# A two-layer decoder on one core: the delta rule's gates in one batch, and another order in its last eight steps

## The chip, the cores and the metric

The kernel runs on one core of one Trainium2 chip. The time is the device time of one launch in microseconds. A profiled execution gives the trace that the rows below are taken from.

## The reference, cut to what matters

Sixteen sequences of 112 tokens and 256 columns go through two decoder layers. The change lies in the first part of the first layer, a gated delta rule with eight heads of 128 columns:

```python
mixed = causal_conv4(x @ qkv_w.T)            # q, k, v: 8 heads x 128
z, bb, aa = x @ z_w.T, x @ b_w.T, x @ a_w.T
beta = sigmoid(bb)
alpha = exp(-exp(A_log) * softplus(aa + dt_bias))
for t in range(T):                           # per sequence and head
    S = S * alpha[t]
    S = S + outer(k[t], (v[t] - k[t] @ S) * beta[t])
    o[t] = q[t] @ S
o = o * rsqrt(mean(o * o) + 1e-6) * norm_w * silu(z)
out = o.reshape(16, 112, 1024) @ out_w.T
```

Behind it come a cross attention, a mixture of eight experts, then in the second layer an attention, a cross attention and a feed-forward part.

## The kernel before, in words

The step over time is turned into matrix products. For each sequence and head, a 112 x 112 matrix of decays (gamma: exp of differences of running sums of the log gates, with log beta added) multiplies k k^T to give N0 and k q^T to give QG. With the inverse of the unit triangular matrix of N0 the output follows. The inverses of the 14 x 14 diagonal blocks (paired to 28 x 28) are worked out on VectorE; the rest is solved by a short series of products, called M, R, Y1, Y2, Y3.

The work is cut into 32 units: eight heads, each with four groups of four sequences (G = 4, 448 columns). Unit u belongs to head u // 4 and group u % 4. The keys part runs eight units ahead (AHEAD = 8) of the solving part. So there is a start, in which units 0 to 7 get their keys, a main loop of 24 steps (u = 0 to 23), each of which solves unit u, finishes the tail of unit u - 1, prepares the values of unit u + 1 and the keys of unit u + 8, and eight last steps (u = 24 to 31) without a keys part. Step 31 begins the cross attention in place of unit 32's values. Every engine's order is written out by hand, and engines wait for each other by semaphores with counts; an engine takes its instructions in that order, so whatever stands behind a waiting instruction waits too. SP issues nearly all DMAs in one queue, with the same effect.

What the steps of the prediction touch:

- The start (gdn_pe, gdn_act, gdn_dve, gdn_pool): for each group, TensorE transposes the normalised rows (start_pe_turn), ScalarE copies them (start_act_copy), TensorE projects 16 gate columns (start_pe_gates), ScalarE copies these (start_act_gates, L455), TensorE turns them back to tokens (start_pe_tokens). Then for a batch of two groups: gate input on VectorE (L361, L362), soft plus on ScalarE (L461 to L468, with a load of the table for Ln and another for Exp behind it), gate output on VectorE (L370, L373), running sums on TensorE (L393, L394), their copy and DMA to memory on ScalarE (L400, L402), and the bias of the sums on VectorE (L381).
- The decays of a unit a: SP fetches its running sums, spread to 112 partitions (cumulative, L1208); logs(a) on GpSimd adds the bias and takes the minimum with zero (L1147, four instructions, into a tile of their own); ScalarE takes the exponential (L838); gammas(a) on GpSimd masks it (L1156); VectorE multiplies it in (N0 at L976, QG at L982).
- The convolutions of keys, queries and values are three instructions each on VectorE (L956) behind ScalarE's tap (L830, L833, L844).
- Inversion and exchange of a head: SP writes N0's diagonal blocks (L1219), gathers them (L1241), VectorE inverts (rows, L536 to L567), SP exchanges the inverses (L1252 to L1264), two joins on GpSimd (join parts 0 and 2, L580) alternate with two on VectorE (parts 1 and 3, L592, L600), and SP writes and spreads the joined blocks (L1270, L1277). Product M of the head's first unit (L672) waits for them. For heads 1 to 7 this goes on inside the steps: joins in the step two ahead of the head's first (u = 2, 6, ..., 26), and in the last eight steps part 0 stands in step 25.
- A step's tail: ScalarE squares the output (L869), GpSimd takes the root (L1160, L1162), ScalarE scales (scale_out, L876), TensorE transposes (L719), VectorE gates (L1018), TensorE projects (L728), VectorE adds to x (L1025). Values: projections L608 (slot 6 for v, slot 8 for z), transposes L657, copy to W0 L852, gate z L992.

## Time and profile before

| | us |
|---|---|
| median of 3 runs | 1888.66 |
| lowest, highest | 1886.35, 1888.81 |
| the profiled execution's own time | 1888.68 |
| its span in the trace | 1887.0 |
| TensorE busy (matmul) | 1806.5 (96%) |
| VectorE busy | 1174.6 (62%) |
| ScalarE busy | 709.8 (38%) |
| GpSimd busy | 669.4 (35%) |

The span runs from the first to the last instruction of the trace; the execution's own time is 1.68 us longer. A busy share is a mean over all stages: the delta rule ends at about 563 us, and what a change in it is worth is read from the stage that it lies in. An idle time in brackets is that of the engine just before the row, with what ended it. In the trace's names, big_a, big_b, h_w, w, expert_w and small are tiles that several stages share; ps is PSUM.

### The profile page before, as it was taken

Reading aid. Unit: us, or ns where it says so; the run is one execution under the profiler, and the core shown is the slowest. Engines: PE = TensorE matmul, PEld = TensorE weight load, DVE = VectorE, ACT = ScalarE, POOL = GpSimd, SP = SyncE. Lnnn points to the kernel's source line nnn. Section 1 sums busy time; section 2 is a strip of 40 time slices with the busy share of each in tenths; the row PEclk is TensorE's granted clock in tenths of the full one; section 3 lists DMA queues with packets and bytes.
Section 4 is the critical chain, followed back from the end, with each engine's and each line's share of the span. In section 5 each row is a group of like instructions: output and inputs, shape, how many; then the busy total and the mean of one; then the engine's idle time right before and its main releaser. Section 6 shows DMA issues by size and latency. Waiting matters only on the chain.

```text
span 1887.0 us, 39461 instructions
## 1 busy us (share of the span) xinstructions
PE 1806.5 (96%) x14800; PEld 1302.7 (69%) x14800; DVE 1174.6 (62%) x3215; ACT 709.8 (38%) x1887; POOL 669.4 (35%) x758
## 2 busy tenths in 40 slices
PE   6679999999889999999999999999999999999999
PEld 3357777776666666665445666666659979889698
DVE  5588888887656677677766667666665234243332
ACT  4124444444345555553001455655632222122221
POOL 3344443443216666674000376676624000000000
PEclk9879999999999999999999999999999999999999
DMA  6312212121022001010000000010040000000000
GB/s 195 53 33 49 39 34 43 37 42 26 13 79 71 25 27 36 26 35 11 1 1 1 10 29 20 20 29 20 11 179 1 3 7 1 10 1 1 10 1 10
DMA packets 98717, 58.61 MB, mean 31 GB/s; under 512 B 77801, under 2 KB 90465, under 8 KB 97761
## 3 DMA queue, kind: packets, MB, share of 16 engines
q1 hardware_dynamic: 98368, 56.03, 11.1%
q8 instruction: 120, 1.97, 0.4%
q14 instruction: 69, 0.56, 0.1%
q10 hardware_dynamic: 160, 0.06, 0.0%
HBM read 50.55 MB, written 5.51 MB: 30 GB/s over the span
## 4 chain that ended last, share of the span: by engine, by line
PE 81%; issue 5%; POOL 5%; DVE 4%; ACT 3%; DMA 1%; SPq 1%; DVEq 0%; POOLq 0%; ACTq 0%
PE ps L2582 18%; PE ps L1566 6%; PE ps L608 6%; PE ps L2454 5%; PE ps L1588 5%; PE ps L2114 5%; PE ps L1604 4%; PE ps L1643 4%; PE ps L1622 4%; PE ps L2660 3%; PE ps L728 2%; POOL w L580 2%; PE ps L1709 2%; PE ps L1575 2%; PE ps L1654 1%
## 5 line engine op out<-in xcount | busy, mean ns | idle before, releaser
L2027 POOL TENSOR_TENSOR h_w<-h_w 125x336 int32<-125x336 int32 x384 | 335.9, 904 | 210.4 <-ACT h_w L1808 210.4
L1912 DVE CUSTOM_DVE_ANT_0 h_w<-ps,h_w 112x375 f32<-112x375 f32 x512 | 263.3, 544 | 0.6 <-issue 0.3
L956 DVE SCALAR_TENSOR_TENSOR big_b<-ps,taps,big_b 128x444 f32<-128x444 f32 (+2 forms) x288 | 194.0, 674 | 74.9 <-ACT big_b L830 47.9
L1808 ACT ACTIVATE h_w<-ps 125x336 f32<-125x336 f32 x512 | 197.7, 468 | 21.7 <-PE ps L1588 21.7
L275 POOL TENSOR_TENSOR rstd<-var_eps,minus_half 112x4 f32<-112x4 f32 x12 | 12.2, 1015 | 406.5 <-DVE var_eps L262 406.5
L1588 PEld LDWEIGHTS ps<-h_w 32*125 32x125 f32 x3072 | 96.0, 183 | 62.1 <-issue 61.3
L1588 PE MATMUL ps<-h_w 32*125 32x112 f32 x3072 | 118.0, 282 | 7.8 <-DVE h_w L1912 5.5
L1921 DVE TENSOR_TENSOR h_w<-h_w,ps 128x112 f32<-128x112 f32 x128 | 34.7, 271 | 141.6 <-PE ps L1575 141.6
L1566 PE MATMUL ps<-h_w 32*112 32x375 f32 x1024 | 121.1, 519 | 0.8 <-DVE h_w L1912 0.8
L608 PE MATMUL ps<-h_w,w 128*128 128x448 f32 x256 | 110.3, 554 | 4.6 <-ACT h_w L852 4.6
L608 PE MATMUL ps<-h_w,kq_w 128*128 128x448 f32 x256 | 113.7, 569 | 0.0
L2114 PE MATMUL ps<-expert_w,big_a 128*112 128x512 f32 x256 | 113.6, 596 | 0.0
L1604 PE MATMUL ps<-h_w 125*32 125x112 f32 x3072 | 101.3, 264 | 0.5 <-POOL h_w L2027 0.4
L2454 PE MATMUL ps<-xT,w 128*128 128x448 f32 x256 | 98.0, 541 | 1.1 <-DVE big_a L2469 1.1
L1156 POOL TENSOR_TENSOR big_a<-big_a,minus_upto 112x448 f32<-112x448 f32 x32 | 36.4, 1136 | 148.5 <-ACT big_a L838 148.5
L2225 DVE SCALAR_TENSOR_TENSOR x<-ps,small,x 112x256 f32<-112x256 f32 x128 | 61.9, 483 | 37.0 <-PE ps L2114 34.0
L2114 PEld LDWEIGHTS ps<-expert_w,big_a 128*112 128x112 f32 x256 | 43.9, 177 | 57.5 <-issue 48.0
L1931 DVE TENSOR_TENSOR h_w<-h_w 125x336 f32<-125x336 f32 x128 | 81.9, 640 | 2.5 <-ACT h_w L1808 2.4
L2454 PEld LDWEIGHTS ps<-xT,w 128*128 128x128 f32 x256 | 48.6, 191 | 46.8 <-issue 44.9
L1604 PEld LDWEIGHTS ps<-h_w 125*32 125x32 f32 x3072 | 70.2, 109 | 15.6 <-issue 1.2
L2582 PE MATMUL ps<-big_b,h_w 128*128 128x224 f32 x384 | 79.1, 353 | 0.0
L2582 PE MATMUL ps<-big_a,h_w 128*128 128x224 f32 x384 | 78.5, 353 | 0.0
(360 smaller groups left out, 3728.9 us busy)
## 6 DMA issues: line engine op xcount, KB each, us to landing
h_w<-in_h SPq DMA_DIRECT2D x2, 4096.0 KB, 17.0
kq_w<-in_ctxT SPq DMA_DIRECT2D x16, 375.0 KB, 3.4
h_w<-in_ctxT SPq DMA_DIRECT2D x16, 375.0 KB, 3.3
big_a<-decays SPq DMA_DIRECT2D x16, 196.0 KB, 3.2
w<-decays SPq DMA_DIRECT2D x16, 196.0 KB, 3.1
h_w<-in_mask SPq DMA_DIRECT2D x16, 164.1 KB, 3.3
kq_w<-in_kq_w SPq DMA_DIRECT2D x8, 256.0 KB, 3.7
w<-in_vz_w SPq DMA_DIRECT2D x8, 256.0 KB, 3.6
```

The lines of the kernel that those rows point to most:

```text
L608: ins = pe.matmul(ps[:, bank, 0:GT], w[:, c, :], c_in[:, c, :], start=(c == 0), stop=(c == KD - 1))
L956: dve.scalar_tensor_tensor(p3(dst)[:, :, i:], p3(ps[:, bank, 0:GT])[:, :, 0:T - i], k.taps[:, h, n, TAPS - 1 - i:TAPS - i], p3(dst)[:, :, ...
L1566: pe.matmul(ps[0:T, score_bank(Q, r), 0:S2], k.Qz[n % 2][rows, z, m, :], k.Kx[n % 2][rows, z, m, :], start=True, stop=True).then_inc(s["S" ...
L1588: ins = pe.matmul(ps[0:CK, turned_bank(Q, r), c * T:(c + 1) * T], k.Kx[n % 2][rows, z, m, c * CK:(c + 1) * CK], k.Qx[Q % 2][rows, :], star ...
L1604: ins = pe.matmul(ps[32 * r:32 * r + 32, 6, q * T:(q + 1) * T], k.Vx[n % 2][:, c, 4 * q + r, :], k.PTx[(4 * Q + r) % RING][:, c * T:(c + 1 ...
L1808: act.activation(k.PTx[(4 * Q + r) % RING], ps[0:CK, turned_bank(Q, r), 0:NC * T], ACT.Exp).then_inc(s["exp"], 1)
L1912: dve.tensor_tensor_reduce(k.masked[r % 2], ps[0:T, score_bank(Q, r), 0:S2], k.mask_add[n % 2], -1.0, 3.0e38, ALU.add, ALU.min, k.neg_max[ ...
L1931: dve.tensor_tensor(P, P, k.mask_I[n % 2], ALU.min).then_inc(s["weights0"], 1)
L2027: pool.tensor_tensor(P.bitcast(I32), P.bitcast(I32), k.mask_I[n % 2], ALU.mult).then_inc(s["weights"], 1)
L2114: ins = pe.matmul(ps[0:T, bank, :], k.moe_xT[g % 2][:, c, j * T:(j + 1) * T], k.expert_w[:, c, e * D:(e + 2) * D], start=(c == 0), stop=(c ...
L2454: ins = pe.matmul(k.ps[:, 2 + 2 * n + m % 2, 0:GT], k.w12[:, n, c, m * 128:(m + 1) * 128], k.xT[:, c, :], start=(c == 0), stop=(c == KD - 1))
L2582: ins = pe.matmul(ps[:, product_bank(p, m), FIRST_HALF], lhsT, rhs, start=(c == 0), stop=(c == QT - 1))
```

## The change

The gates of all sixteen sequences are worked out in one batch. All four groups' turns, copies and gate projections come ahead of unit 0's first tap on ScalarE, and gate input, soft plus, gate output, running sums, their write and the bias run once on 128 columns instead of twice on 64. ScalarE takes unit 0's query tap behind the soft plus. The logs of a unit are one tensor_tensor and one tensor_scalar over 448 columns, in place in the fetched sums, instead of four tensor_scalars of 112 columns into another tile. In the start GpSimd takes logs(a + 1) ahead of gammas(a). SP's fetch waits for the exponential of the unit two back instead of its logs.

In the last eight steps TensorE takes z's projection, Y2, v's projection, the tail's transposes and M behind Y1, where it took v's projection, the transposes, Y2, z's projection and M. ScalarE takes A ahead of the scaling and z ahead of v. VectorE takes less, the gate and the R sum ahead of the values' convolution, M and z.

The diff, cut to its core:

```diff
-BATCH = 2 * G
+ALL = B * HEADS
...
 
 def turn_banks(g):
-    return (5, 0) if g == 1 else (3, 4)
+    return (5, 0) if g % 2 else (3, 4)
...
-def start_dve_gate_in(dve, k, s, b):
+def start_dve_gate_in(dve, k, s):
     (y, t1, t2, bb), _, _, _, _ = start_tiles(k)
-    dve.wait_ge(s["ba_t"], 2 * b + 2)
-    if b == 0:
-        dve.wait_ge(s["c_ba"], 48)
-    for g in (2 * b, 2 * b + 1):
+    dve.wait_ge(s["c_ba"], 48)
+    for g in range(NG):
+        dve.wait_ge(s["ba_t"], g + 1)
         ba = k.ps[0:T, gate_bank(g), GT:GT + G * 16].rearrange("p (g c) -> p g c", g=G)
-        at = slice(G * (g % 2), G * (g % 2) + G)
-        dve.tensor_tensor(y[:, b, at, :], ba[:, :, HEADS:], k.dt_bias[:, :].unsqueeze(1).to_broadcast([T, G, HEADS]), ALU.add)
-        ins = dve.tensor_copy(bb[:, b, at, :], ba[:, :, 0:HEADS])
+        at = slice(G * g, G * g + G)
+        dve.tensor_tensor(y[:, at, :], ba[:, :, HEADS:], k.dt_bias[:, :].unsqueeze(1).to_broadcast([T, G, HEADS]), ALU.add)
+        ins = dve.tensor_copy(bb[:, at, :], ba[:, :, 0:HEADS])
     ins.then_inc(s["ba_in"], 1)
...
+def start_dve_gate_out(dve, k, s):
     (y, t1, t2, bb), _, _, _, _ = start_tiles(k)
-    at = slice(BATCH * b, BATCH * b + BATCH)
-    dve.wait_ge(s["soft_plus"], nth(b, 5, 4))
-    dve.scalar_tensor_tensor(t2[:, b], y[:, b], 0.0, t1[:, b], ALU.max, ALU.add).then_inc(s["gates"], 1)
-    dve.wait_ge(s["gates"], nth(b, 3, 0))
+    dve.wait_ge(s["soft_plus"], 4)
+    dve.scalar_tensor_tensor(t2, y, 0.0, t1, ALU.max, ALU.add).then_inc(s["gates"], 1)
+    dve.wait_ge(s["gates"], 1)
     dve.wait_ge(s["setup_act"], 1)
-    dve.scalar_tensor_tensor(k.gate_rows[:, 1, b], t2[:, b].rearrange("p s h -> p h s"), -1.0,
-                             k.decay[:, :].unsqueeze(2).to_broadcast([T, HEADS, BATCH]), ALU.mult, ALU.mult).then_inc(s["gates"], 1)
...
+def start_dve_bias(dve, k, s):
 
     (y, t1, t2, bb), _, _, _, _ = start_tiles(k)
-    dve.wait_ge(s["cum_ps"], 2 * b + 1)
-    dve.scalar_tensor_tensor(k.gate_rows[:, 0, b], bb[:, b].rearrange("p s h -> p h s"), -1.0,
-                             k.ps[0:T, 6, 0:BATCH * HEADS].rearrange("p (h s) -> p h s", h=HEADS), ALU.mult, ALU.subtract).then_inc(s["gates"], 1)
-
-
-def start_pe_cum(pe, k, s, b):
-
-    pe.wait_ge(s["gates"], nth(b, 3, 1))
-    if b:
-        pe.wait_ge(s["cum_sb"], b)
-    else:
-        pe.wait_ge(s["ba_in"], 1)
-    g = k.gate_rows[:, 1, b].rearrange("p h s -> p (h s)")
-    pe.matmul(k.ps[0:T, 6, 0:BATCH * HEADS], k.upto[:, :], g, start=True, stop=True).then_inc(s["cum_ps"], 1)
-    pe.matmul(k.ps[0:BATCH * HEADS, 5, 0:T], g, k.upto[:, :], start=True, stop=True).then_inc(s["cum_ps"], 1)
-
-
-def start_act_cum(act, k, s, b):
-
-    act.wait_ge(s["cum_ps"], 2 * b + 2)
-    act.activation(k.cum_rows[b], k.ps[0:BATCH * HEADS, 5, 0:T], ACT.Copy).then_inc(s["cum_sb"], 1)
-    act.wait_ge(s["cum_sb"], b + 1)
-    act.dma_start(k.cum_d[b].rearrange("h s t -> (h s) t"), k.cum_rows[b]).then_inc(s["cum_w"], 16)
+    dve.wait_ge(s["cum_ps"], 2)
+    dve.wait_ge(s["soft_plus"], 5)
+    dve.scalar_tensor_tensor(k.gate_rows[:, 0], bb.rearrange("p s h -> p h s"), -1.0,
+                             k.ps[0:T, 6, 0:ALL].rearrange("p (h s) -> p h s", h=HEADS), ALU.mult, ALU.subtract).then_inc(s["gates"], 1)
+
+
+def start_pe_cum(pe, k, s):
+
+    pe.wait_ge(s["gates"], 2)
+    g = k.gate_rows[:, 1].rearrange("p h s -> p (h s)")
+    pe.matmul(k.ps[0:ALL, 5, 0:T], g, k.upto[:, :], start=True, stop=True).then_inc(s["cum_ps"], 1)
+    pe.matmul(k.ps[0:T, 6, 0:ALL], k.upto[:, :], g, start=True, stop=True).then_inc(s["cum_ps"], 1)
+
+
+def start_act_cum(act, k, s):
+
+    act.wait_ge(s["cum_ps"], 1)
+    act.activation(k.cum_rows, k.ps[0:ALL, 5, 0:T], ACT.Copy).then_inc(s["setup_act"], 1)
+    act.wait_ge(s["setup_act"], 2)
+    act.dma_start(k.cum_d.rearrange("h s t -> (h s) t"), k.cum_rows).then_inc(s["cum_w"], 16)
...
+def start_act_soft_plus(act, k, s):
...
 def gdn_pe(pe, k, s):
...
     start_pe_turn(pe, k, s, 0)
     start_pe_gates(pe, k, s, 0)
     start_pe_turn(pe, k, s, 1)
+    start_pe_tokens(pe, k, s, 0)
+    start_pe_gates(pe, k, s, 1)
+    start_pe_turn(pe, k, s, 2)
+    start_pe_tokens(pe, k, s, 1)
+    start_pe_gates(pe, k, s, 2)
     keys(0, 0)
-    start_pe_turn(pe, k, s, 2)
-    start_pe_gates(pe, k, s, 1)
+    start_pe_turn(pe, k, s, 3)
+    start_pe_tokens(pe, k, s, 2)
+    start_pe_gates(pe, k, s, 3)
     keys(0, 2)
-    start_pe_tokens(pe, k, s, 0)
-    start_pe_tokens(pe, k, s, 1)
-    start_pe_turn(pe, k, s, 3)
+    start_pe_tokens(pe, k, s, 3)
     keys(1, 0)
     keys(0, 4)
     pe.wait_ge(s["c_gdn"], 96)
-    start_pe_cum(pe, k, s, 0)
-    start_pe_gates(pe, k, s, 2)
+    start_pe_cum(pe, k, s)
     keys(1, 2)
-    start_pe_gates(pe, k, s, 3)
-    start_pe_tokens(pe, k, s, 2)
-    start_pe_tokens(pe, k, s, 3)
     keys(0, 10)
     keys(1, 4)
     keys(2, 0)
     keys(1, 10)
     keys(2, 2)
-    start_pe_cum(pe, k, s, 1)
...
         solve(u, "Y1")
         if more:
+            values(u + 1, 8)
+            solve(u, "Y2")
             values(u + 1, 6)
+            tail(u - 1, 2)
+            solve(u + 1, "M")
         else:
             pe.wait_ge(s["sz"], UNITS)
             cross_head_pe(pe, k, s, 0, 0)
-        tail(u - 1, 2)
-        solve(u, "Y2")
-        if more:
-            values(u + 1, 8)
-            solve(u + 1, "M")
+            solve(u, "Y2")
+            tail(u - 1, 2)
         solve(u, "Y3")
...
 def gdn_act(act, k, s):
...
-            act.wait_ge(s["logs"], a + 1)
+            act.wait_ge(s["logs"], 2 * a + 2)
             if a:
                 act.wait_ge(s["gam"], a)
-            act.activation(k.gamma, k.soft[0:T, :, :].rearrange("p g t -> p (g t)"), ACT.Exp).then_inc(s["gamma"], 1)
+            act.activation(p3(k.gamma), k.cum[a % 2], ACT.Exp).then_inc(s["gamma"], 1)
...
     start_act_gates(act, k, s, 0)
     start_act_copy(act, k, s, 1)
+    start_act_gates(act, k, s, 1)
+    start_act_copy(act, k, s, 2)
+    start_act_gates(act, k, s, 2)
+    start_act_copy(act, k, s, 3)
+    start_act_gates(act, k, s, 3)
     act.wait_ge(s["c_gdn"], 96)
     keys(0, 0)
-    start_act_copy(act, k, s, 2)
-    start_act_gates(act, k, s, 1)
+    start_act_soft_plus(act, k, s)
     keys(0, 2)
-    start_act_soft_plus(act, k, s, 0)
-    keys(1, 0)
-    start_act_cum(act, k, s, 0)
-    start_act_copy(act, k, s, 3)
+    start_act_cum(act, k, s)
     act.wait_ge(s["setup_pool"], 1)
     exp_table()
-    start_act_gates(act, k, s, 2)
+    keys(1, 0)
     keys(1, 2)
     keys(0, 3)
-    start_act_gates(act, k, s, 3)
     keys(1, 3)
-    start_act_soft_plus(act, k, s, 1)
     keys(2, 0)
-    exp_table()
     keys(2, 2)
-    start_act_cum(act, k, s, 1)
     keys(2, 3)
...
-        more = is_unit(u + 1)
+        solve(u, "A")
         scale_out(u - 1)
-        solve(u, "A")
-        if more:
+        if is_unit(u + 1):
+            values(u + 1, 8)
             values(u + 1, 6)
-            values(u + 1, 8)
             solve(u + 1, "R")
...
 def gdn_dve(dve, k, s):
...
-    start_dve_gate_in(dve, k, s, 0)
+    start_dve_gate_in(dve, k, s)
     keys(0, 3)
-    start_dve_gate_out(dve, k, s, 0)
+    start_dve_gate_out(dve, k, s)
     for a in range(1, AHEAD + 1):
         for slot in (2, 4, 3, 10):
             if a == 1 and slot == 2:
-                start_dve_bias(dve, k, s, 0)
+                start_dve_bias(dve, k, s)
             elif a == 1 and slot == 4:
                 keys(1, 3)
-            elif a == 3 and slot == 2:
-                start_dve_bias(dve, k, s, 1)
-            if a == 1 and slot == 10:
-                start_dve_gate_in(dve, k, s, 1)
-            elif a == 2 and slot == 2:
-                start_dve_gate_out(dve, k, s, 1)
...
+        solve(u, "less")
         tail(u - 1, 3)
-        solve(u, "less")
+        if not more:
+            cross_head_dve(dve, k, s, 0, 0)
+        solve(u, "R")
         if more:
             values(u + 1, 7)
+            solve(u + 1, "M")
             values(u + 1, 9)
-            solve(u + 1, "M")
-        else:
-            cross_head_dve(dve, k, s, 0, 0)
-        solve(u, "R")
...
 def gdn_pool(pool, k, s):
...
-        b, first = g // 2, G * (g % 2)
-        if a < NG:
-            pool.wait_ge(s["gates"], 3 * (b + 1))
+        if a == 0:
+            pool.wait_ge(s["gates"], 3)
         pool.wait_ge(s[f"cum_in{a % 2}"], 16 * (a // 2 + 1))
-        if a:
-            pool.wait_ge(s["gamma"], a)
-        for j in range(G):
-            ins = pool.tensor_scalar(k.soft[0:T, j, :], k.cum[a % 2][:, j, :], k.gate_rows[:, 0, b, h, first + j:first + j + 1], 0.0,
-                                     ALU.add, ALU.min)
-        ins.then_inc(s["logs"], 1)
+        cum = k.cum[a % 2]
+        pool.tensor_tensor(cum, cum, k.gate_rows[:, 0, h, G * g:G * g + G].unsqueeze(2).to_broadcast([T, G, T]), ALU.add).then_inc(s["logs"], 1)
+        pool.wait_ge(s["logs"], 2 * a + 1)
+        pool.tensor_scalar(cum, cum, 0.0, None, ALU.min).then_inc(s["logs"], 1)
...
     for a in range(AHEAD):
+        logs(a + 1)
         gammas(a)
-        logs(a + 1)
...
 def gdn_sp(sp, k, s, a):
...
-        first = G * (g % 2)
-        if unit in (0, 2):
-            sp.wait_ge(s["cum_w"], 16 * (g // 2 + 1))
+        if unit == 0:
+            sp.wait_ge(s["cum_w"], 16)
         if unit >= 2:
-            sp.wait_ge(s["logs"], unit - 1)
-        sp.dma_start(k.cum[unit % 2], k.cum_d[g // 2, h, first:first + G].unsqueeze(0).to_broadcast([T, G, T])).then_inc(s[f"cum_in{unit % 2}"], 16)
+            sp.wait_ge(s["gamma"], unit - 1)
+        sp.dma_start(k.cum[unit % 2], k.cum_d[h, G * g:G * g + G].unsqueeze(0).to_broadcast([T, G, T])).then_inc(s[f"cum_in{unit % 2}"], 16)
```

## Rows read from the trace of the kernel before

**Rows 1.** The page, part 4: chain that ended last, by engine.

```profile
PE 81%; issue 5%; POOL 5%; DVE 4%; ACT 3%; DMA 1%; SPq 1%; DVEq 0%; POOLq 0%; ACTq 0%
```

**Rows 2.** Windows: stretch, length, busy PE, PEld, DVE, ACT, POOL, clock, DMA.

```profile
0.00:118.00 118.00, 73.75 (x297) 44.91 (x298) 69.14 (x155) 31.57 (x60) 43.05 (x56) 0.84 0.42 106
118.00:467.00 349.00, 344.64 (x2287) 249.57 (x2286) 294.85 (x537) 149.78 (x474) 150.53 (x176) 1.00 0.20 38
467.00:546.00 79.00, 71.74 (x505) 53.72 (x503) 46.17 (x88) 31.63 (x112) 13.93 (x14) 1.00 0.09 19
```

**Rows 3.** Timeline, start: start us, us, engine line op, names [idle before].

```profile
20.82 2.10 DVE L956 SCALAR_TENSOR_TENSOR big_b<-ps,taps,big_b 128x444 f32<-128x444 f32 x3 [1.41 <-ACT big_b L830]
...
29.24 0.49 ACTq L402 DMA_DIRECT2D decays<-silu  x1
...
35.19 2.60 POOL L1147 TENSOR_SCALAR soft<-big_a,small 112x112 f32<-112x112 f32 x4 [12.60 <-DMA big_a<-decays]
...
38.30 0.52 ACT L455 ACTIVATE big_b<-ps 16x448 f32<-16x448 f32 x1
...
52.59 2.56 POOL L1147 TENSOR_SCALAR soft<-big_a,small 112x112 f32<-112x112 f32 x4 [8.62 <-issue]
...
66.05 0.61 DVE L976 TENSOR_TENSOR h_w<-ps,big_a 112x448 f32<-112x448 f32 x1
...
87.86 0.43 SPq L1208 DMA_DIRECT2D big_a<-decays  x1
...
91.13 2.56 POOL L1147 TENSOR_SCALAR soft<-big_a,small 112x112 f32<-112x112 f32 x4 [20.03 <-DMA big_a<-decays]
...
111.94 1.76 PE L672 MATMUL ps<-expert_w,h_w 112*112 112x84 f32 x8 [0.66 <-DMA expert_w<-joined]
...
117.95 0.76 PE L686 MATMUL ps<-big_a 112*84 112x84 f32 x8
```

**Rows 4.** Lines by form, GpSimd: count, busy us, mean ns, idle before.

```profile
L1147 POOL TENSOR_SCALAR soft<-w,small 112x112 f32<-112x112 f32 x64 | 41.2, 662 | 0.0
...
L1156 POOL TENSOR_TENSOR big_a<-big_a,minus_upto 112x448 f32<-112x448 f32 x32 | 36.4, 1136 | 148.5 <-ACT big_a L838 148.5
...
L2034 POOL TENSOR_SCALAR h_w<-h_w 112x375 f32<-112x375 int32 x16 | 24.0, 1500 | 1.4
...
L1160 POOL TENSOR_SCALAR var_eps<-var_eps 112x4 f32<-112x4 f32 x32 | 8.0, 251 | 123.8 <-ACT xn L869 123.3
```

**Rows 5.** Timeline: loop step u = 2 with a join, and the next.

```profile
152.52 2.58 POOL L1147 TENSOR_SCALAR soft<-w,small 112x112 f32<-112x112 f32 x4
...
159.43 1.14 ACT L876 ACTIVATE xn<-ps,rstd 112x128 f32<-112x128 f32 x4 [0.58 <-POOL rstd L1162]
...
163.28 1.04 PE L630 MATMUL ps<-big_b 128*112 128x112 f32 x8 [0.49 <-DVE big_b L956]
```

**Rows 6.** Windows and timeline of the undisturbed late step 28.

```profile
512.39:523.75 11.36, 10.30 (x74) 7.70 (x73) 5.49 (x10) 4.60 (x19) 1.26 (x2) 1.00 0.01 1
...
513.92 1.74 PE L608 MATMUL ps<-h_w,w 128*128 128x448 f32 x4 [0.77 <-ACT h_w L852]
...
515.95 0.60 PE L719 MATMUL ps<-ident,xn 112*128 112x112 f32 x4 [0.29 <-ACT xn L876]
```

**Rows 7.** Timeline: the joins of head 7 in the last eight steps.

```profile
487.13 2.88 POOL L580 TENSOR_TENSOR w<-w 128x1372 f32<-128x1372 f32 x1 [6.50 <-issue]
...
502.06 1.68 SPq L1277 DMA_DIRECT2D expert_w<-joined  x4
...
507.27 0.93 PE L672 MATMUL ps<-expert_w,h_w 112*112 112x84 f32 x8
```

**Rows 8.** Timeline: TensorE after 5.6 us idle, and in the loop.

```profile
58.48 1.84 PE L630 MATMUL ps<-big_b 128*112 128x112 f32 x8 [5.63 <-DVE big_b L956]
...
60.10 3.22 PE L608 MATMUL ps<-h_w,kq_w 128*128 128x448 f32 x4
...
148.23 1.04 PE L630 MATMUL ps<-big_b 128*112 128x112 f32 x8
```

More of the change, by code:

```diff
@@ L151, in memory @@
     k.On = k.xn[:, 0:2, :].rearrange("p a b -> p (a b)")
[L152 to L153 removed]
+    k.gate_rows = k.small[:, 0:8, :].rearrange("p a b -> p (a b)").rearrange("p (n h s) -> p n h s", n=2, h=HEADS)
+    k.cum_rows = k.silu[:, :, :].rearrange("p a b -> p (a b)")[:, 2 * GT - T:2 * GT]
     k.gate_cols = [k.big_b[0:16, n, :] for n in (3, 5)]
@@ L303, in start_tiles @@
     flat = k.silu[0:T, :, :].rearrange("p a b -> p (a b)")
-    n = 2 * BATCH * HEADS
-    gates = [flat[:, i * n:(i + 1) * n].rearrange("p (b s h) -> p b s h", b=2, s=BATCH) for i in range(4)]
+    n = ALL
+    gates = [flat[:, i * n:(i + 1) * n].rearrange("p (s h) -> p s h", h=HEADS) for i in range(4)]
     mean_var = flat[:, 4 * n:4 * n + 2 * B].rearrange("p (s c) -> p s c", c=2)
@@ L427, in start_pe_gates @@
         pe.wait_ge(s["c_ba"], 48)
-    turned = g + 1 if g < 2 else NG
-    pe.wait_ge(s["lnT_act"], turned)
-    pe.wait_ge(s["lnT_dve"], turned)
+    pe.wait_ge(s["lnT_act"], g + 1)
+    pe.wait_ge(s["lnT_dve"], g + 1)
     for c in range(KD):
```

35 lines of the change are left out of this document (16 added, 19 removed).

## The prediction, made before the changed kernel ran

> **What bounds the kernel now.** I read the chain of work that ended last first: four fifths of it are TensorE's [rows 1], so only what keeps TensorE waiting can be won or lost. The busy time by stretch then says where that is [rows 2]. From 0 to 118 us TensorE works 73.75 of 118 us: the start. From 118 to 467 us, in the 24 steps of the main loop, it works 344.64 of 349 us. From 467 to 546 us, the last eight steps of the delta rule, 71.74 of 79 us. Behind 563 us the change touches nothing. So the reader is to see three places: a start that is bound by waits, a loop that has a few tenths to give, and a tail with 7 us of waits.
>
> In the start the timeline shows the chain [rows 3]: key convolution of unit 0 at 20.82, running sums written out at 29.24, their read back and the first logs at 35.19. Unit 2's logs wait until 52.59 for the second batch of gates (8.62 us idle). The fourth N0 comes at 66.05; then the blocks go through memory, the inversion and the exchange, which SP's queue works off in order, so that the sums of unit 6 are fetched only at 87.86 and GpSimd stands still for 20.03 us until 91.13. The first big product starts at 111.94.
>
> **The change, part 1: one batch of gates in the start.** It removes one pass of gate input, soft plus, two activation table loads, gate output, running sums and a DMA out and in, all on engines that wait in that stretch, and the 8.62 us wait with it. It costs a later first pass. All four groups are now turned and projected before ScalarE taps unit 0's keys: three more groups at some 3.4 us each (gate product, ScalarE's copy of it, copies of the next group; a ScalarE copy is 0.52 [rows 3]). By my walk ScalarE is through with them at about 29 us and the key convolution of unit 0 (2.10) runs at 29.6 instead of 20.82. Behind it on VectorE stands the gate input (31.7); on ScalarE the soft plus (32.6 to 35.2) now stands ahead of unit 0's query tap, and on VectorE the query convolution, which waits for that tap, stands ahead of the gate output. So the output comes at 38, the sums are written at 39.6, and the first logs run at 45 instead of 35.19: 10 us later. From the write at 29.24 to these logs it is 5.95 us now [rows 3]; I take 5.5 in a quieter queue.
>
> What comes after catches up: no second batch, so logs of unit 2 at about 51 (now 52.59). From there VectorE sets the pace (two convolutions of 2.10 and two products of 0.61 a unit, 5.4 us) and the fourth N0 comes at 68 instead of 66.05. Inversion and exchange are unchanged and carry this on: fetch of unit 6's sums at about 89.7 against 87.86, its logs 91.13 plus 1.9.
>
> **Part 2: GpSimd's order and SP's wait.** logs(a+1) now stands ahead of gammas(a). While the sums arrive in time this costs nothing, and twice they don't. Gammas of unit 5, done long before the 20 us wait now, would stand behind logs of unit 6. N0 and the kept product of unit 5 with them, VectorE's joins for head 0 behind these: 1.3 us more, so the first big product at 115.2 against 111.94. The second time is logs of unit 8, whose fetch stands behind the joined blocks in SP's queue: gammas of unit 7, and so the product that TensorE needs for R of step 0, come 5 us later than now. SP's fetches wait for the exponential of the unit two back instead of its logs, as the sums are now changed in place; in the loop the fetch then lands over 10 us ahead of its use, since SP is held by N0 of the unit before anyway. Sum for the start: about +5 us at step 0, +3 at best, +9 at worst (see the price of the new logs).
>
> **Part 3: the logs themselves.** Four tensor_scalars of 112 columns (2.56 us together at 52.59 [rows 3]) become a tensor_tensor and a one-input tensor_scalar on 448 columns. The first has its row: same shape, 1136 ns [rows 4]. The second isn't in the trace. From below it can't cost less than one of today's quarters, 662 ns; from above, L2034 (two operations, one input, 375 columns) took 1500 ns, which is 1.79 us for 448. I take 1.14, the row of the same width with one operation on each element. So 2.28, bounds 1.80 to 2.93. The Trainium skill ("GPSIMD Engine Reference", "3.1 Elementwise — side-by-side cycle accounting") says that a one-input body of up to two operations runs at 1.03 cycles an element against about 2.6 with two inputs; by that the second would cost about as little as the lower bound. From 4 to 375 columns L1160 and L2034 differ by 1249 ns [rows 4], 3.4 ns a column, which speaks for the upper bound at two operations; no row has one operation on many columns of one input.
>
> In the loop this counts only where the joins are: logs lie between two joins, and the root behind them releases ScalarE, which waited 0.58 us for it (159.43), and TensorE, which waited 0.49 us (163.28) [rows 5]. Such a step comes for heads 1 to 6: 6 x -0.28 = -1.7 us, bounds 6 x -0.58 = -3.5 and 6 x +0.37 = +2.2. In the other steps GpSimd waits for ScalarE: zero; its cover would be gone only with some 3 us more a step.
>
> **Part 4: the last eight steps.** In an undisturbed step TensorE works 10.30 of 11.36 us [rows 6], and waits twice: 0.77 us with the value projection for ScalarE's copy of the step before (513.92), and 0.29 us with the transposes for the scaled output (515.95). With the pipeline's drain at both I count 1.35. The new order puts the z projection and Y2 ahead of these two; walking all queues with the durations of such a step, I find both waits gone and the tightest remaining one (the gated output ahead of the output projection) 0.4 us early, so the step is 10.0 us. Six step starts, from step 25's to step 31's, could gain 8.1 us.
>
> But two are lost to the joins of head 7. In step 24 VectorE now has its convolution behind the R sum, so the inversion's end slips by 2.6 us, while the steps are shorter. On GpSimd the first join (487.13, 2.88 us [rows 7]) then runs 489.8 to 492.7, and step 25's root is queued behind it: transposes in step 26 wait 3.2 us. Then the last join stands behind z's product on VectorE, and the joined blocks, spread by SP at 502.06 now with TensorE asking at 507.27 [rows 7], land at 507.7 where TensorE asks at 505.8: 1.9 us. 8.1 - 5.1 = 3.0, with 0.2 in the last step -3.2 us; bounds -5 and -1.
>
> **Sum.** +5.0 - 1.7 - 3.2 = +0.1 us. The profiled execution took 1888.68 us with a span of 1887.0, the median is 1888.66: the same base. Forecast 1889 us. Less than 0.2% (3.8 us) can't be told from no change in a measurement of this kernel.
>
> **Rivals.** First, slower: the clock. The new TensorE waits (6 us for the running sums, 3.2 us in step 26, 1.9 us in step 28) make the granted clock fall to its lower level (1.2 instead of 2.4 GHz). The price has rows [rows 8]: after 5.63 us idle the eight small products of L630 took 1.84 against 1.04 us, and the four of L608 3.22 against 1.74: 2.3 us for a fall. My walk has such a fall in the start where TensorE idles longest, none in the tail. With all three: 1888.8 + 6.9 = 1895.7; it decides from the second one on. For it: the rows. Against: 1.06 us of waits a step left the clock at 1.00 [rows 6], and the wait for the blocks absorbs part. The Trainium skill ("TensorE: Matmul & The Clock Gate", "Why this matters for your kernels") asks for no long idle gaps between bursts of matmuls, or the clock goes back to half; by it the change is a loss at these places. Chance 0.2.
>
> Second, slower: the new tensor_scalar costs its upper bound. Logs take 2.93: start +8, loop +2.2, tail -3.2, 1895.7. Against: one operation, not two. 0.1.
>
> Third, faster: it costs its lower bound, 0.66 us, with half the operations of L1147's. Start +3, loop -3.5, tail -3.2: 1885.0. Against it stands the slope above. Chance 0.17; half of that lies within 0.2%. The rule of the Trainium skill on one-input bodies, named in part 3, would make this the case.
>
> Fourth, the tail does all that it is meant to, with the joins in time: 1888.7 + 5 - 1.7 - 9.6 = 1882.4. Against: the queues of VectorE and GpSimd would have to bring the joins earlier than my walk has them. 0.08.
>
> **Chances.** Forecast 0.45, the rivals 0.55. The forecast's own errors (start 2 us, tail 1.5 us) give faster and slower 0.05 each. Faster: 0.08 + 0.09 + 0.05 = 0.22. Slower: 0.2 + 0.1, less a third of it that stays in the band, + 0.08 for what a walk overlooks = 0.28. Same 0.5. Range 1882.5 to 1896.5, which takes in all cases up to their middles.
>
> **What would show it.** Right: first logs near 45 us; the 8.62 us wait gone; a wait of 20 us before logs of unit 6 with gammas of unit 5 behind it; first Y1 (117.95 now, [rows 3]) near 123; tensor_scalar of 448 columns near 1.1 us; last undisturbed steps 10.0 us apart; waits of 3 and 2 us in steps 26 and 28. Wrong: a first Y1 by 118 or past 127; a tensor_scalar outside 0.66 to 1.79; steps still 11.4 apart; a half clock in the tail.

## The result and the profile after

| | us |
|---|---|
| before, median of 20 runs beside the changed kernel | 1885.99 (1884.48 to 1889.54) |
| changed kernel, median of 20 runs | 1889.25 (1886.29 to 1892.27) |
| ratio, 95% interval | 1.0015 [1.0009, 1.0021] |
| span of the profiled execution, before and after | 1887.0, 1888.5 |

The change costs 0.15%, 2.8 us by the ratio: it lies on the slow side of zero and within the 0.2% that the prediction called no change. The forecast was 1889.0, but part of that agreement is luck: the sum was +0.1 us on a base of 1888.66, and the base measured again over 20 runs is 2.7 us lower.

The chain of the changed kernel, by engine, and the same three stretches by windows (stretch, length, busy PE, PEld, DVE, ACT, POOL, clock, DMA share, GB/s). The stretches end at 120, 472 and 550 us, where [rows 2] have 118, 467 and 546, as the start now takes longer:

```profile
PE 80%; DVE 5%; POOL 5%; issue 4%; ACT 2%; DMA 2%; SPq 1%; DVEq 0%; POOLq 0%; ACTq 0%
```

```profile
0.00:120.00 120.00, 73.54 (x282) 42.72 (x283) 67.32 (x151) 27.98 (x50) 40.10 (x38) 0.84 0.39 102
120.00:472.00 352.00, 348.82 (x2293) 251.86 (x2293) 295.61 (x539) 150.55 (x475) 143.16 (x130) 0.99 0.20 38
472.00:550.00 78.00, 75.02 (x525) 57.35 (x524) 46.62 (x89) 33.16 (x122) 13.59 (x16) 0.96 0.10 20
```

The start does the same work with more waiting than in [rows 2]. In the tail TensorE is busy for all but 3 of 78 us, against 7 of 79 before, but its granted clock has fallen from 1.00 to 0.96, so part of that busy time is slow work.

The timeline of the start, after (start, us, engine, line, operation, names, idle before):

```profile
18.98 3.14 PE L426 MATMUL ps<-h_w,ba_w 128*16 128x448 f32 x4 [0.24 <-ACT h_w L442]
...
31.80 2.10 DVE L947 SCALAR_TENSOR_TENSOR big_b<-ps,taps,big_b 128x444 f32<-128x444 f32 x3 [12.05 <-ACT big_b L825]
...
41.87 0.34 ACTq L397 DMA_DIRECT2D decays<-silu  x1
...
46.90 0.93 POOL L1129 TENSOR_TENSOR big_a<-big_a,small 112x448 f32<-112x448 f32 x1 [23.97 <-DMA big_a<-decays]
...
65.07 0.93 POOL L1129 TENSOR_TENSOR big_a<-big_a,small 112x448 f32<-112x448 f32 x1 [3.49 <-DMA big_a<-decays]
...
70.39 0.61 DVE L967 TENSOR_TENSOR h_w<-ps,big_a 112x448 f32<-112x448 f32 x1
...
92.06 0.43 SPq L1189 DMA_DIRECT2D big_a<-decays  x1
...
95.31 0.93 POOL L1129 TENSOR_TENSOR big_a<-big_a,small 112x448 f32<-112x448 f32 x1 [21.41 <-DMA big_a<-decays]
...
97.62 1.13 POOL L1138 TENSOR_TENSOR big_a<-big_a,minus_upto 112x448 f32<-112x448 f32 x1
98.71 2.88 POOL L575 TENSOR_TENSOR w<-w 128x1372 f32<-128x1372 f32 x1
...
117.34 1.76 PE L667 MATMUL ps<-expert_w,h_w 112*112 112x84 f32 x8 [0.62 <-DMA expert_w<-joined]
...
124.30 1.06 PE L681 MATMUL ps<-big_a 112*84 112x84 f32 x8
```

Against [rows 3]: first key convolution at 31.80 instead of 20.82, first logs at 46.90 instead of 35.19, fourth N0 at 70.39 instead of 66.05, fetch of unit 6 at 92.06 instead of 87.86, first M at 117.34 instead of 111.94, first Y1 at 124.30 instead of 117.95. Behind the wait of 21.41 us stand unit 6's logs, then unit 5's gammas (97.62), then the join. The 8.62 us wait is gone.

The new logs by form, beside the gammas (count, busy us, mean ns, idle before):

```profile
L1138 POOL TENSOR_TENSOR big_a<-big_a,minus_upto 112x448 f32<-112x448 f32 x32 | 36.4, 1137 | 144.5 <-ACT big_a L833 124.9 <-DMA w<-inverses 13.1 <-DMA w<-inverses_t 6.6
L1131 POOL TENSOR_SCALAR big_a<-big_a 112x448 f32<-112x448 f32 x16 | 21.4, 1335 | 1.4
...
L1129 POOL TENSOR_TENSOR w<-w,small 112x448 f32<-112x448 f32 x16 | 15.0, 935 | 3.8 <-DMA w<-decays 3.8
```

The timeline of the tail, with two windows of it, one in step 26 and one in an undisturbed step:

```profile
494.80 2.87 POOL L575 TENSOR_TENSOR w<-w 128x1372 f32<-128x1372 f32 x1 [9.29 <-issue]
497.75 0.23 POOL L1142 TENSOR_SCALAR var_eps<-var_eps 112x4 f32<-112x4 f32 x1
...
500.33 0.99 PE L714 MATMUL ps<-ident,xn 112*128 112x112 f32 x4 [2.69 <-ACT xn L871]
501.11 1.66 PE L667 MATMUL ps<-expert_w,h_w 112*112 112x84 f32 x8
...
515.10 1.98 PE L723 MATMUL ps<-gdn_out_w,big_b 128*112 128x256 f32 x8
```

```profile
502.50:507.00 4.50, 4.50 (x20) 3.37 (x20) 3.62 (x7) 0.00 (x0) 0.00 (x0) 0.50 0.01 4
513.00:523.00 10.00, 10.00 (x73) 7.62 (x72) 5.53 (x10) 4.61 (x17) 1.27 (x2) 1.00 0.02 2
```

An undisturbed step has no wait and takes 9.89 us (10.30 of 11.36 us were busy before, [rows 6]). Step 26 takes 15.99 (a step runs from its Y1 to the next step's): 2.69 us of wait for the root that stands behind the first join, and then 3.4 us because the clock stands at 0.50 for a while and the products behind it take up to twice as long.

By the first product Y1 of each step, read in both traces:

| stage | before | after | difference |
|---|---|---|---|
| start, to Y1 of step 0 | 117.95 | 124.30 | +6.35 |
| loop, to Y1 of step 24 | 349.80 | 348.94 | -0.86 |
| tail, to Y1 of step 31 | 78.73 | 75.44 | -3.29 |
| step 31, and what follows to the end of the span | 1340.5 | 1339.8 | -0.7 |
| span | 1887.0 | 1888.5 | +1.5 |

The start takes different times in different executions of the same instructions, and some kernels below share one of the two starts. The start of before is in e1_late_alone and e10_inverse_early too: first Y1 at 115.61 and 116.11, with 117.95 here. The changed start is in e2_start_alone and e6_root_first too: 121.98 and 122.61, with 124.30 here. Both executions of the pair are the late ones of their three; the means, 116.6 and 123.0, are 6.4 apart, so the +6.35 stands.

### The profile page after: what moved, and what is told of

Read it like the earlier page. It is cut to its first block, busy times and chain, and to the rows that moved or that the text cites. A ratio compares the mean times of both kernels' runs of the same rounds, so it can differ in the third digit from the quotient of the medians.

```text
span 1888.5 us, 39343 instructions
## 1 busy us (share of the span) xinstructions
PE 1810.5 (96%) x14796; PEld 1304.0 (69%) x14796; DVE 1173.3 (62%) x3212; ACT 707.7 (37%) x1878; POOL 659.3 (35%) x694
## 4 chain that ended last, share of the span: by engine, by line
PE 80%; DVE 5%; POOL 5%; issue 4%; ACT 2%; DMA 2%; SPq 1%; DVEq 0%; POOLq 0%; ACTq 0%
PE ps L2563 18%; PE ps L1547 6%; PE ps L603 5%; PE ps L2435 5%; PE ps L1569 5%; PE ps L2095 5%; PE ps L1585 4%; PE ps L1624 4%; PE ps L1603 4%; PE ps L2641 3%; PE ps L723 2%; POOL w L575 2%; PE ps L1690 2%; PE ps L1556 2%; DVE big_b L947 2%
```

## The experiments

The theory: the start loses some 5 us or more, mostly by GpSimd's order; the logs give 1 to 2 us; the tail gives some 3 to 4 and leaves the rest to the joins of head 7. The rivals: the price of the clock, another price of the logs, a tail that gives all. Each was timed against before in its own session (4 to 12 executions of the kernel). The sessions differ, so a difference between two kernels below is that of their ratios, at 1886 us, and not of their medians. An interval is about 0.1% wide to either side, 2 us, so a difference of 2 us between two kernels is not clear of it.

| kernel | median us | ratio to before [95%] |
|---|---|---|
| changed kernel | 1889.25 | 1.0015 [1.0009, 1.0021] |
| e1_late_alone | 1883.46 | 0.9981 [0.9973, 0.999] |
| e2_start_alone | 1892.1 | 1.0033 [1.0021, 1.0045] |
| e3_gammas_first | 1882.89 | 0.9978 [0.9969, 0.9987] |
| e4_new_logs | 1884.9 | 0.9989 [0.998, 0.9998] |
| e5_tap_first | 1887.45 | 1.0004 [0.9994, 1.0014] |
| e6_root_first | 1889.55 | 1.0015 [1.0006, 1.0024] |
| e7_early_fetch | 1876.65 | 0.995 [0.9938, 0.9963] |
| e8_all | 1872.32 | 0.9919 [0.9907, 0.9931] |
| e10_inverse_early | 1881.73 | 0.9971 [0.9961, 0.9982] |
| e11_three | 1872.67 | 0.9926 [0.9914, 0.9938] |
| e9_best | 1869.58 | 0.9906 [0.9893, 0.992] |

### The two halves, each alone

The first is the kernel before with the tail's new order (shown for TensorE; ScalarE and VectorE go with it), the second the changed kernel with the tail's old one.

```diff
         solve(u, "Y1")
         if more:
-            values(u + 1, 6)
+            values(u + 1, 8)
+            solve(u, "Y2")
+            values(u + 1, 6)
+            tail(u - 1, 2)
+            solve(u + 1, "M")
         else:
             pe.wait_ge(s["sz"], UNITS)
             cross_head_pe(pe, k, s, 0, 0)
-        tail(u - 1, 2)
-        solve(u, "Y2")
-        if more:
-            values(u + 1, 8)
-            solve(u + 1, "M")
+            solve(u, "Y2")
+            tail(u - 1, 2)
```

> Before with the last eight steps' new order alone. Theory 1 (three separate sums, from the two traces: start +6.3 us at step 0, loop -0.9, tail -3.8): the first Y1 stays at 118 us, steps 25, 27 to 30 are 9.9 us long instead of 11.4, step 26 is about 16 us with the lower clock level in it, and the time is 3.8 us below before (ratio 0.998). Rival (the tail's gain in the trace is a matter of where the stages happen to meet, and most of it goes when the start is not moved): within 1 us of before.

> The changed kernel with the last eight steps in the old order. Theory 1: first Y1 near 124.3 us, steps of 11.4 us in the tail, 5.5 us above before (ratio 1.0029), and the sum of this run's and the late order's difference is the whole change's. Rival (the tail owes part of its gain to the new start): the tail's last step starts at the same distance from its first as in before, but the time is 3 us or less above before.

Measured: -0.19% (3.6 us) and +0.33% (6.2 us). They add up to +0.14%, the whole of the change. So the near zero is a loss and a gain that cancel, not two parts that do nothing. The start of the tail alone, which is the start of before in another execution, and TensorE in its step 26:

```profile
33.48 2.61 POOL L1147 TENSOR_SCALAR soft<-big_a,small 112x112 f32<-112x112 f32 x4 [11.71 <-DMA big_a<-decays]
...
109.87 1.76 PE L672 MATMUL ps<-expert_w,h_w 112*112 112x84 f32 x8 [0.73 <-DMA expert_w<-joined]
...
115.61 0.76 PE L686 MATMUL ps<-big_a 112*84 112x84 f32 x8
...
492.71 0.60 PE L719 MATMUL ps<-ident,xn 112*128 112x112 f32 x4 [2.79 <-ACT xn L877]
...
494.47 3.48 PE L728 MATMUL ps<-gdn_out_w,big_b 128*112 128x256 f32 x8
```

The wait is there without the new start, so it belongs to the new order. Step 26 took 14.52 us here and not 15.99: the clock fell again, but for a shorter while (1.8 us beside the wait, where it was 3.4), and M in step 27 then waited 0.64 us for its blocks.

### GpSimd's order in the start

The changed kernel, with gammas ahead again:

```diff
-        logs(a + 1)
         gammas(a)
+        logs(a + 1)
```

> The changed kernel with GpSimd's order of the start undone: gammas(a) ahead of logs(a+1). Theory 1 (gammas stand behind logs that wait for their fetch, at units 5 and 7): gammas of unit 5 run before the 21 us wait, first Y1 near 119.5 us instead of 124.3, 4 to 5 us less than the changed kernel, so 1 to 2 us below before. Rival (the later first logs, 46.9 us instead of 35.2, carry through to step 0 whatever the order is): first Y1 stays above 123 us and the time within 1 us of the changed kernel's.

Measured: 0.9978 against 1.0015, 7.0 us less. Its start, and TensorE in steps 26 and 27:

```profile
18.24 1.66 PE L426 MATMUL ps<-h_w,ba_w 128*16 128x448 f32 x4 [0.26 <-ACT h_w L442]
...
44.74 0.93 POOL L1129 TENSOR_TENSOR big_a<-big_a,small 112x448 f32<-112x448 f32 x1 [22.55 <-DMA big_a<-decays]
...
92.24 0.93 POOL L1129 TENSOR_TENSOR big_a<-big_a,small 112x448 f32<-112x448 f32 x1 [19.90 <-DMA big_a<-decays]
...
94.55 2.86 POOL L575 TENSOR_TENSOR w<-w 128x1372 f32<-128x1372 f32 x1
...
112.56 1.76 PE L667 MATMUL ps<-expert_w,h_w 112*112 112x84 f32 x8 [0.64 <-DMA expert_w<-joined]
...
117.75 0.76 PE L681 MATMUL ps<-big_a 112*84 112x84 f32 x8
...
493.38 0.60 PE L714 MATMUL ps<-ident,xn 112*128 112x112 f32 x4 [2.80 <-ACT xn L871]
495.01 1.98 PE L723 MATMUL ps<-gdn_out_w,big_b 128*112 128x256 f32 x8
...
506.09 1.76 PE L667 MATMUL ps<-expert_w,h_w 112*112 112x84 f32 x8 [2.22 <-issue]
508.29 3.76 PE L723 MATMUL ps<-gdn_out_w,big_b 128*112 128x256 f32 x8
```

The join now follows the logs at once (94.55 against 92.24, 2.3 us; it was 3.4 us with gammas in between), and from M to Y1 of step 0 it is 5.19 us instead of 6.96. From the first logs to the first Y1 it is 73.01 against 77.40: 4.4 us that the order costs. The other 2.2 of the 6.55 us at Y1 are first logs that came earlier, where this edit touches nothing: the second group's gate product (L426) took 1.66 us here and 3.14 in the profiled execution of the changed kernel. The double time speaks for a clock that rose later there, but this is inferred: the view's granted clock is 1.00 at that place in both. Two other kernels with the same start up to there have their first logs at 44.58 and 44.66, so 46.90 is that execution's, not the change's; the 35.19 of before is late in the same way, with 33.48 and 33.58 in e1_late_alone and e10_inverse_early. In the medians the order is worth 7 us, more than the 4.4. What the rest is stays open; the profiled execution (1885.05) is one of the longest of its twelve (1879.81 to 1885.46), so others must have lost less somewhere, and no trace shows where.

In the tail this execution has both waits that were forecast, 2.80 us in step 26 with the clock held, and 2.22 in step 27 with a fall behind it. Steps 26 and 27 took 12.91 and 15.45 us, together 2.4 more than the 15.99 and 9.93 of the changed kernel, where the fall in step 26 gave the blocks time to land.

### The new logs alone

The kernel before with the logs' new form and its waits, gates in two batches, order as before:

```diff
-        for j in range(G):
-            ins = pool.tensor_scalar(k.soft[0:T, j, :], k.cum[a % 2][:, j, :], k.gate_rows[:, 0, b, h, first + j:first + j + 1], 0.0,
-                                     ALU.add, ALU.min)
-        ins.then_inc(s["logs"], 1)
+        cum = k.cum[a % 2]
+        pool.tensor_tensor(cum, cum, k.gate_rows[:, 0, b, h, first:first + G].unsqueeze(2).to_broadcast([T, G, T]), ALU.add).then_inc(s["logs"], 1)
+        pool.wait_ge(s["logs"], 2 * a + 1)
+        pool.tensor_scalar(cum, cum, 0.0, None, ALU.min).then_inc(s["logs"], 1)
```

> Before with the new form of the logs alone (one tensor_tensor and one tensor_scalar over 448 columns in place, SP's fetch behind the exponential), gates in two batches and the old orders. Theory 1: 2.35 us a unit instead of 2.57; 0.5 us less in the start, 6 x 0.15 to 0.2 in the loop's join steps, nothing else: 1.5 us below before (ratio 0.9992). Rival (SP's later fetch costs in the start what the form saves): first Y1 at or above 118 us, time within 0.5 us of before.

Measured: -0.11%, 2.1 us, with 1.5 expected. From Y1 of step 0 to Y1 of step 24 it takes 348.97 us against 349.80. Nine of the kernels here with the new logs lie between 348.27 and 349.42 there, four with the old between 349.74 and 350.11: 1.2 us in the loop by the means. The interval (0.998 to 0.9998) leaves 0.4 to 3.8 us for the whole, so that the form gives something is shown, and how much is not.

### ScalarE's tap ahead of the soft plus

```diff
     keys(0, 0)
-    start_act_soft_plus(act, k, s)
     keys(0, 2)
+    start_act_soft_plus(act, k, s)
     start_act_cum(act, k, s)
```

> The changed kernel with ScalarE's tap of unit 0's queries ahead of the soft plus. Theory 1 (part of the late start is that VectorE's query convolution waits 3.3 us for this tap and the gate output stands behind it): the convolution runs under the soft plus, first logs 2.5 us earlier (44.4 instead of 46.9), first Y1 2 to 2.6 us earlier than 124.3, time 2 to 2.5 us below the changed kernel. Rival (only the queue behind GpSimd's order counts, the first logs have slack): first Y1 within 0.5 us of 124.3.

Measured: 1.0004 against 1.0015, 2.1 us less, and the first logs come 2.6 us ahead of the 44.58 that the same start with the tap behind the soft plus has:

```profile
42.00 0.93 POOL L1129 TENSOR_TENSOR big_a<-big_a,small 112x448 f32<-112x448 f32 x1 [20.16 <-DMA big_a<-decays]
```

Its first Y1 comes at 119.73, with 121.98 and 122.61 in the two traces above that share the start with the tap behind (e2_start_alone, e6_root_first). So that tap was on the way of the gates, as the prediction had it, and 2.6 us of the first logs' delay are this order and not the batching itself. The intervals of the two ratios overlap; it is the traces that show it.

### The root ahead of the join in the tail

```diff
         if u > UNITS - AHEAD:
             root(u - 1)
         if h2 is not None:
+            join(pool, k, s, h2, 0)
             join(pool, k, s, h2, 2)
-        if h3 is not None:
-            join(pool, k, s, h3, 0)
```

with VectorE's join part 1 moved behind the gate.

> The changed kernel, head 7's joins moved: on GpSimd both joins behind step 25's root, on VectorE join part 1 behind the gated output of step 26. Theory 1 (step 26 is 16 us long because that root stood behind a join that waited for its data, and the clock fell in the wait): step 26 is about 10 us, step 27 about 12.8 with TensorE waiting for the joined blocks, the time 2 to 4 us below the changed kernel; if the clock falls in step 27's wait instead, 1 us below. Rival (step 26's length is the inversion's and the exchange's, not the queue's): step 26 stays above 14 us, no gain.

Measured: 1.0015, no gain. The theory of where the wait comes from holds; that removing it pays does not. The profiled execution:

```profile
492.14 0.23 POOL L1142 TENSOR_SCALAR var_eps<-var_eps 112x4 f32<-112x4 f32 x1 [8.58 <-ACT xn L864]
...
508.84 0.99 PE L667 MATMUL ps<-expert_w,h_w 112*112 112x84 f32 x8 [2.64 <-issue]
510.10 1.98 PE L723 MATMUL ps<-gdn_out_w,big_b 128*112 128x256 f32 x8
```

The root runs on time, step 26 takes 10.11 us, and a wait of nearly the same size, 2.64 us, comes in the next step ahead of M, which waits for the joined blocks. This execution took 1883.62, the shortest of its twelve, with its clock at 1.00 behind the wait (L723 1.98 us); the median is 1889.55, at a mean clock of 0.985 to 0.986 in most executions against 0.987 here. In e8_all, with the same two edits, the clock fell at this place:

```profile
493.54 1.76 PE L667 MATMUL ps<-expert_w,h_w 112*112 112x84 f32 x8 [3.23 <-issue]
495.74 3.63 PE L723 MATMUL ps<-gdn_out_w,big_b 128*112 128x256 f32 x8
```

Its step 27 took 15.94 us. That most executions of e6_root_first fall likewise is what the medians and mean clocks suggest; no trace shows such a one, so why the edit gains nothing in the median stays open.

### The inversion of head 7 earlier

The tail alone, and the inversion on VectorE moved ahead: its rows 4 to 6 (of the blocks, not of the groups above) between less and the gate of step 24, its last rows ahead of the sum into x.

```diff
             rows_first(dve, k, s, h3)
+            tail(u - 2, 5)
         if h2 is not None:
             join(dve, k, s, h2, 1)
         solve(u, "less")
+        if h4 is not None:
+            rows(h4, range(4, 7))
         tail(u - 1, 3)
 ...
-        if h4 is not None:
-            rows(h4, range(4, 7))
         if h2 is not None:
             join(dve, k, s, h2, 3)
-        tail(u - 1, 5)
+        if h4 is None:
+            tail(u - 1, 5)
```

> The kernel before with the new order of the last eight steps, and in step 24 the inversion of head 7 put ahead: rows 4 to 6 stand between less and the gate, the last rows ahead of the sum into x. Theory 1 (the 2.8 us wait of step 26 at the transposes is step 25's root queued behind the first join of head 7, which waits for the inversion): the first join starts about 3 us earlier against the step's first product, the wait at the transposes in step 26 goes below 0.5 us, and the wait for the joined blocks in step 27 stays 1 to 2.5 us, as the last join is bound by its place behind z on VectorE. Total 1 to 3.4 us below the 1883.5 of the new order alone, some 1881. Theory 2 (the wait has another source, such as ScalarE's order): the wait stays 2.8 us and the time 1883.5.

Measured: 0.9971 against 0.9981, 1.9 us less by the ratios, whose intervals overlap (0.9961 to 0.9982 and 0.9973 to 0.999). The trace is clearer:

```profile
485.30 2.89 POOL L580 TENSOR_TENSOR w<-w 128x1372 f32<-128x1372 f32 x1 [6.64 <-issue]
...
490.85 0.60 PE L719 MATMUL ps<-ident,xn 112*128 112x112 f32 x4 [0.63 <-ACT xn L877]
...
503.16 0.99 PE L672 MATMUL ps<-expert_w,h_w 112*112 112x84 f32 x8 [1.82 <-issue]
504.41 3.30 PE L728 MATMUL ps<-gdn_out_w,big_b 128*112 128x256 f32 x8
```

The wait at the transposes went from 2.79 to 0.63 us as the inversion came forward (the join by 2.2 us against the step's Y1; 3 were expected), so the chain inversion, join, root is the cause. The wait for the joined blocks is 1.82 us, the size that the prediction gave it, and the clock falls there instead (step 27 takes 13.60 us).

### The fetch of unit 6 ahead of the exchange

[Rows 3] show the longest wait of the start, 20.03 us on GpSimd for sums that SP had not asked for, since their fetch stood behind the exchange of head 0. This edit of the kernel before moves that one fetch, and nothing else:

```diff
-            if is_unit(unit + 2):
+            if is_unit(unit + 2) and unit != NG:
                 cumulative(unit + 2)
 ...
         if h is not None:
+            if h == 0:
+                cumulative(NG + 2)
             exchange(h)
```

> Before with one move on SP: the fetch of unit 6's sums ahead of the exchange of head 0. Theory 1 (the 20 us wait of GpSimd for these sums, and all behind it, is only SP's order): logs of unit 6 at about 75 us instead of 91, first Y1 9 us earlier (109), time 8 to 10 us below before (ratio 0.995). Rival (the exchange and the joins set the end of the start; the 20 us are slack that they cover): first Y1 not more than 2 us earlier.

Measured: 0.995, 9.4 us less.

```profile
69.95 0.65 SPq L1208 DMA_DIRECT2D big_a<-decays  x1
...
74.13 2.94 POOL L1147 TENSOR_SCALAR soft<-big_a,small 112x112 f32<-112x112 f32 x4 [5.30 <-DMA big_a<-decays]
...
82.70 2.86 POOL L580 TENSOR_TENSOR w<-w 128x1372 f32<-128x1372 f32 x1 [5.63 <-DMA w<-inverses_t]
...
101.20 1.65 PE L672 MATMUL ps<-expert_w,h_w 112*112 112x84 f32 x8
...
106.00 0.76 PE L686 MATMUL ps<-big_a 112*84 112x84 f32 x8
```

The join waits for its own blocks instead of for logs that stand ahead of it, and the first Y1 comes at 106.00 instead of 117.95. Against the two other traces with the start of before (115.61 and 116.11) that is 9.6 to 10.1 us, which fits the 9.4 of the runs better than 12 does.

### All together, with one batch and with two

The first is the changed kernel with the four edits on its start, joins and fetch shown above. The second is the kernel before with the tail's order, the new logs and the early fetch, and its two batches of gates kept. The third is the second with the early inversion.

```diff
 e8_all    = changed kernel + e3_gammas_first + e5_tap_first + e6_root_first + e7_early_fetch
 e11_three = kernel before + e1_late_alone + e4_new_logs + e7_early_fetch
 e9_best   = e11_three + e10_inverse_early
```

> The changed kernel with four moves: gammas ahead of logs in GpSimd's start, the tap ahead of the soft plus, head 7's joins behind the root, the fetch of unit 6 ahead of the exchange. Theory 1 (each wait is of its own queue, so the gains add): first Y1 at 105 to 108 us with 124.3 in the changed kernel, the tail 3 us shorter, time about 19 us below the changed kernel, 16 below before (ratio 0.9915). Rival (they are the same wait seen from several queues): less than 12 us below the changed kernel.

> The kernel before with three things: the new order of the last eight steps (measured alone -3.6 us), the new form of the logs (-2.1) and the early fetch of unit 6's sums (-9.4). It keeps the gates in two batches. Theory 1 (the one batch of gates brings nothing of its own once the fetch is early, since inversion and exchange of head 0 end at the same time either way): the three add up, 15 us below before, about 1871 for a before of 1886, equal to or a little under the kernel with one batch and all other mends (1872.3). Theory 2 (the one batch is worth something): 1874 or more.

> The three things of the run beside it and the early inversion of head 7. Theory 1: 1 to 3.4 us below that run, about 1869. Theory 2 (the tail's wait only moves to the joined blocks, or the clock falls there): no more than 0.5 us below it.

Measured: 0.9919, 0.9926 and 0.9906, so 15.3, 14.0 and 17.7 us below before, with 16 and 15 expected for the first two: the gains nearly add up. The first two can't be told apart in time, and their first Y1 comes at 106.76 and 105.12. So no gain of the one batch shows once the fetch is early; whether it costs something is not settled, since the two kernels also differ in head 7's joins. The third is the shortest kernel of all, 20.6 us below the changed kernel; its lead on the second is 3.8 us by the ratios (1 to 3.4 expected), whose intervals just overlap. What is left in its tail is a wait of 0.94 us in step 26 and 1.80 in step 27, with a fallen clock behind the second (step 27 takes 13.57 us).

## Why the prediction was right, and where it was not

**Start.** Forecast +5 at step 0, range +3 to +9; the pair of traces gives +6.35, the means of three traces of each start +6.4. The mechanism was right at each point: the key convolution (29.6 forecast; 31.80 in the late profiled execution, 28.92 to 29.50 in five others with this start), first logs (45; 46.90, and 44.58 to 44.74 in three), the long wait with unit 5's gammas behind it, the late gammas of unit 7 (117.21) that R of step 0 waits for. The later first pass was taken to carry 1.9 us through to the fetch of unit 6, and about that came: e3_gammas_first has it without the order, and its M starts at 112.56 against 109.87 and 110.30 in e1_late_alone and e10_inverse_early, its Y1 at 117.75 against 115.61 and 116.11, so 1.6 to 2.7 us later. (Against the profiled execution of before, 111.94 and 117.95, it would look like nothing, but that is the late one of its three.) The term that was mis-sized is GpSimd's order: taken at 1.3 us ahead of M and 1.8 behind it, it is 2.6 (70.44 against 67.82, measured from the first logs) and 1.8. The step of the prediction that failed is the sentence that only twice the sums don't arrive in time: the trace has waits of 1.9 to 3.5 us for them at units 3, 4 and 5 too (65.07), and behind each stand the gammas of the unit before, which VectorE needs for the kept product.

**Logs.** Forecast 1.14 + 1.14 us; measured 0.93 + 1.33, from one start to the next 2.34 with the gaps. Two misses cancelled: the tensor_tensor was read off a row with the same shape but another operand, and the one-input instruction lay above the row chosen, as the slope in [rows 4] had said, and inside the bounds. The Trainium skill's rule named in the prediction ("GPSIMD Engine Reference", "3.1 Elementwise — side-by-side cycle accounting"), by which a one-input body takes fewer cycles an element than one with two inputs, is not what this trace shows: from 4 columns (228 ns) to 448 (1335 ns) it is 2.5 ns a column, not under the two-input instruction but over it. The loop gave 0.9 us of the 1.7 forecast in this pair, 1.2 by the means of all traces.

**Tail.** Forecast -3.2; measured -3.8 up to the last root, -3.3 up to the last Y1, and -3.6 in the run with the tail alone. The undisturbed step is 9.89, forecast 10.0, and both waits of [rows 6] are gone. The joins cost what was forecast, but not as forecast. Step 26 waits 2.69 us (3.2 forecast), and then the clock falls, which the prediction had as a rival (2.3 us a fall) and its own walk didn't hold. The fall took 3.4 us, and in the changed kernel it covered the second wait: M in step 27 finds its blocks there. Without the first wait the second appears, at 1.82 and 2.64 us. (The prediction puts it in step 28; it is M of unit 28, which TensorE takes in step 27.) So one pair of 3.2 and 1.9 was forecast, a pair of 2.69 and 3.4 came. A half clock in the tail was one of the prediction's own signs of being wrong, and it came; that the tail's sum still held is luck.

**The rivals.** The clock: it fell at one of the two new places of the tail, not at both, and the second wait of the forecast went into it, so the two steps lost 6.1 us where 5.1 were forecast, and not 9.7. Its price, 2.3 us, lies inside what the falls took: 1.8 or 1.9 us in e1_late_alone, e5_tap_first, e9_best and e10_inverse_early, 2.8 in e8_all, 3.3 to 3.4 in e3_gammas_first, e11_three and the changed kernel (step length less 9.89 and the wait). The Trainium skill ("TensorE: Matmul & The Clock Gate", "Why this matters for your kernels") warns of long idle gaps between bursts of matmuls, behind which the clock goes back to half. In step 26 the granted clock was 0.50 behind a gap of 2.69 us, so the trace has such a fall; but after 2.80 us in e3_gammas_first and 2.64 in e6_root_first it stayed at 1.00, so a gap of this length is no sure fall here. The logs at either bound: 1.33 us lies between. The full tail: the joins were late, as the case against it said. Its price of 9.6 us has no source in the prediction, whose part 4 gives 8.1 and 0.2. In the chances, the 0.28 for slower leaves out the 0.05 of the forecast's own errors.

**The sum.** +0.1 forecast; +1.5 in the spans and +2.8 in the ratio. The terms, +5, -1.7, -3.2, came out as +6.35, -0.86, -3.3 to -3.8. That is the start too small by 1.4 and the loop too large by 0.8. A case for slower by up to 0.2% was in the forecast's own spread, and the 2.8 us are in it.

## What to carry to other kernels

In an engine with a hand-written order, an instruction that waits for a DMA should stand behind all that could already run: two swapped lines on GpSimd cost 4.4 us by the traces and 7 by the runs, and the batching that they came with showed no gain to set against it. Before the work in a slow stage is made cheaper, ask of its longest wait which queue entry holds the transfer back; here one fetch moved ahead of an exchange was worth more than any other edit. And when a wait on a shared chain (inversion, joins, blocks) is removed at one place, follow the chain to its next user before the gain is booked. Last, a start read from one trace of each kernel can be off by 2 us either way; traces of other kernels that share it show how far.
